# One-hot products for tiles 28 to 30 at the seam between attention and experts, and another order on VectorE

## The reference

```python
x = x + hilbert_attention(layernorm(x), Wqkv, bqkv, Wproj, bproj, mapping)       # part 1
x = x + cross_attention(layernorm(x), ctx, Wq, Wkv, null_kv, Wout, scale, bias)  # part 2: 16 heads, 154+1 keys
f = layernorm(x)                                                                 # part 3
probs = softmax(f @ Wr + br); gate = max(probs); idx = argmax(probs)             # 8 experts
pos = cumsum(one_hot(idx)) * one_hot(idx)        # place of a token in its expert's list
keep = pos < 512                                 # capacity 4096 / 8
expert_in[e, pos] = gate * f                     # "dispatch"
h = relu(expert_in @ W1 + b1); eo = h @ W2 + b2
x = x + gate * eo[idx, pos]                      # where kept, else x
```

## Time and profile before

| | us |
|---|---|
| median of 3 runs | 1298.02 (1295.5 to 1300.58) |
| the profiled execution, its own time | 1294.91 |
| its span | 1293.2 |
| PE busy | 1268.1 (98%) |
| DVE busy | 939.7 (73%) |
| ACT busy | 662.4 (51%) |
| POOL busy | 419.9 (32%) |

### The profile page before, as it was taken

One profiled execution on the slowest core, in us unless ns is written; L12 is line 12 of the kernel. 1 busy time (PEld: TensorE's weight loads), 2 busy tenths in 40 slices (PEclk: granted clock), 3 DMA queues, 4 the chain that ended last, 5 costly groups with the idle time before them and its releaser, 6 DMA issues.

```text
span 1293.2 us, 31661 instructions
## 1 busy us (share of the span) xinstructions
PE 1268.1 (98%) x12348; PEld 1032.6 (80%) x12348; DVE 939.7 (73%) x1903; ACT 662.4 (51%) x1868; POOL 419.9 (32%) x477
## 2 busy tenths in 40 slices
PE   9999999999999999999999999999999998999998
PEld 8988677777777788888888888888888876888886
DVE  6559787888886776777777777787767787665563
ACT  4456333433333755656556565565555752654552
POOL 3213454545432021213232132312212222555453
PEclk9999999999999999999999999999999999999999
DMA  8542244444323201103021020120202103664630
GB/s 268 169 132 66 68 157 158 148 151 165 109 83 109 82 10 42 50 18 107 18 75 50 18 105 20 48 77 18 74 18 98 58 26 133 231 208 153 189 99 22
DMA packets 70257, 123.75 MB, mean 96 GB/s; under 512 B 12313, under 2 KB 21553, under 8 KB 70114
## 3 DMA queue, kind: packets, MB, share of 16 engines
q1 hardware_dynamic: 61794, 98.17, 22.8%
q0 software_dynamic: 8320, 23.62, 5.2%
HBM read 83.19 MB, written 42.07 MB: 97 GB/s over the span
## 4 chain that ended last, share of the span: by engine, by line
PE 85%; DVE 9%; ACT 3%; issue 2%; DMA 1%; SPq 1%; POOL 0%; DVEq 0%; POOLq 0%
PE bank L71 20%; PE bank L73 18%; PE bank L72 18%; PE bank L2371 6%; PE bank L2355 6%; PE bank L2394 4%; PE bank L2386 2%; PE bank L1306 2%; PE bank L1276 1%; PE bank L1250 1%; PE bank L2927 1%; PE bank L2445 1%; PE bank L2434 1%; DVE turned_l L1054 1%; DVE a_recip L1060 1%
## 5 line engine op out<-in xcount | busy, mean ns | idle before, releaser
L1655 ACT ACTIVATE b_prob<-bank,b_neg_top 128x155 f32<-128x155 f32 x496 | 186.7, 408 | 115.0 <-DVE b_neg_top L1871 115.0
L1871 DVE TENSOR_REDUCE b_neg_top<-bank 128x6 f32<-128x930 f32 (+1 forms) x93 | 94.2, 1013 | 64.2 <-PE bank L2371 64.2
L71 PE MATMUL bank<-turned_h,big_h 128*128 128x512 f32 x320 | 131.3, 410 | 1.4 <-DVE turned_l L2131 1.2
L73 PE MATMUL bank<-turned_h,big_l 128*128 128x512 f32 x320 | 125.4, 392 | 0.0
L72 PE MATMUL bank<-turned_l,big_h 128*128 128x512 f32 x320 | 124.8, 390 | 0.0
L71 PE MATMUL bank<-b_wo_h,b_ot_h 128*128 128x512 f32 x256 | 111.5, 436 | 1.9 <-ACT b_ws L1688 1.7
L2355 PEld LDWEIGHTS bank<-ident,b_prob 128*128 128x128 f32 x640 | 92.8, 190 | 22.1 <-issue 5.0
L2355 PE MATMUL bank<-ident,b_prob 128*128 128x128 f32 x640 | 104.0, 285 | 3.3 <-DVE b_pt L1888 2.2
L1655 ACT ACTIVATION_READ_ACCUMULATOR b_prob<-bank,b_neg_top 128x1 f32 x496 | 103.9, 209 | 0.0
L73 PE MATMUL bank<-b_wo_h,b_ot_l 128*128 128x512 f32 x256 | 101.1, 395 | 0.0
L72 PE MATMUL bank<-b_wo_l,b_ot_h 128*128 128x512 f32 x256 | 99.9, 390 | 0.0
(11 more groups left out here) (361 smaller groups left out, 3353.7 us busy)
## 6 DMA issues: line engine op xcount, KB each, us to landing
wide<-in_L_ffn_W_dram SPq DMA_DIRECT2D x16, 1024.0 KB, 5.4
slot_rows<-empty_row SPq DMA_DIRECT2D x8, 1032.0 KB, 5.4
a_xr<-in_x_dram SPq DMA_DIRECT2D x32, 256.0 KB, 2.8
x_scratch<-a_xr SPq DMA_DIRECT2D x32, 256.0 KB, 2.4
tiles<-x_scratch SPq DMA_DIRECT2D x32, 256.0 KB, 3.7
rows<-x_scratch SPq DMA_DIRECT2D x32, 256.0 KB, 3.4
out_dram<-rows SPq DMA_DIRECT2D x32, 256.0 KB, 2.0
rows<-slot_rows SPq DMA_DIRECT2D x7, 1032.0 KB, 8.4
```

Of the source, the lines that this page charges most:

```text
L71: pe.matmul(out, lh, rh, start=first, stop=False)
L73: return pe.matmul(out, ll, rh, start=False, stop=last)
L1655: last = act.activation(prob[:, n % 2, j, h:h + 2 * L2 - 1:2], burst_banks(n, b)[:, h, o:o + L2], ACT.Exp, bias=neg_top[:, n % 2, h, j:j + 1],
L1871: dve.tensor_reduce(neg_top[:, n % 2, :, first:end], burst_banks(n, b)[:, :, 0:(end - first) * L2].rearrange("p h (j k) -> p h j k", k=L2) ...
```

## The change

It does the following:
- `queries(1, 3)` is cut in two in step 1: the first six matmuls stand ahead of `turn_p(1, 4)`, the other six at the end.
- y-statistics and logits of tile 28 and `w_stats(29)` on DVE move from the end of step 30 into step 31, behind the copy of the second turn, ahead of `route_slots`.
- SP fetches the rows of expert 0 once tile 27's scatter is done, in step 32. Tiles 28, 29, 30 come in by one-hot products, high part and remainder, as tile 31 does (`own_norm` on ACT, `place_own` for the matrices: 0 and 1 on DVE, 2 on GpSimd; `own_rest` for the remainders: 0 and 1 on GpSimd, 2 on DVE; `pick_own` on PE).
- The scatter of tiles 28 to 30 moves behind that fetch, to GpSimd's step 33.
- `warm` shrinks from seven, a narrow one and two to one; the pieces 4 to 7 of DVE's `expert_split` move behind `first_rest`.

```diff
@@ SP
             if tiled(n - 2):
                 need(sp, s["x2_made"], n - 1)
                 sp.dma_start(out_tiles[:, n - 2, :], row(n - 2)).then_inc(x2_stored[(n - 2) % (2 * G)], 16)
+            if n == NT:
+                sp.wait_ge(s["scattered"], SENT[LAST - 1])
+                for k in range(G):
+                    sp.wait_ge(x2_stored[k], 16 * NT // (2 * G))
+                    sp.dma_start(rows[:, 0, k, :], slot_tiles[:, k, :]).then_inc(first_rows[k], 16)
@@
-        sp.wait_ge(s["scattered"], SENT[LAST])
-        for k in range(G):
-            sp.wait_ge(x2_stored[k], 16 * NT // (2 * G))
-            sp.dma_start(rows[:, 0, k, :], slot_tiles[:, k, :]).then_inc(first_rows[k], 16)
@@ GpSimd
+        def own_rest(k):
+            hold(pool, s["own_high"], k + 1)
+            pool.tensor_tensor(own_l[k], own[k], own_h[k].bitcast(F32), ALU.subtract).then_inc(s["own_low"], 1)
+
+        def place_own(k):
+            m = NT - G + k
+            hold(pool, s["routed"], LAST)
+            hold(pool, s["own_placed"], k)
+            pool.tensor_scalar(own_picked[k], numbers[:, :], token_f[:, m:m + 1], c4["slot4"][:, k:k + 1], ALU.subtract,
+                               ALU.is_equal).then_inc(s["own_placed"], 1)
@@
             if n == NT:
                 power("y", n - 1)
-                scatter(LAST - 1)
+                own_rest(0)
                 power("w", n)
+                own_rest(1)
                 return
             if tiled(n - 2):
                 power("y", n - 1)
             if n == NT + 1:
+                place_own(2)
 
                 for k in range(G):
                     hold(pool, first_rows[k], 16)
+                scatter(LAST - 1)
                 scatter(LAST)
@@ ACT
+        def own_norm(k):
+            need(act, s["route_step"], BASE[LAST - 1] + 13)
+            here = rows[:, (NT - 1) // G % 2, k, :]
+            act.activation(own[k], here[:, 0:D], ACT.Identity, bias=here[:, D + 2:D + 3], scale=here[:, D + 3:D + 4])\
+                .then_inc(s["own_normed"], 1)
+            need(act, s["own_normed"], k + 1)
+            act.activation(own_h[k], own[k], ACT.Copy).then_inc(s["own_high"], 1)
@@
                 turned_y(n - 2)
                 route_exp(LAST - 1)
+                own_norm(0)
                 w_copy(n - 1)
+                own_norm(1)
+                first_norm(0)
+                own_norm(2)
                 turned_y(n - 1)
+                first_norm(1)
+                first_norm(2)
                 route_exp(LAST)
-                first_norm(0)
-                first_norm(1)
+                first_norm(3)
...
-                first_norm(2)
-                first_norm(3)
@@ DVE, closing
             if t == 2:
-                need(dve, s["x2_made"], n - 1)
-                norm_stats("y", n - 1, row(n - 2), EPS1)
                 read_counts(NG - 2)
-            logits(n - 2)
-            if t == 2:
-                w_stats(n - 1)
+            else:
+                logits(n - 2)
@@ DVE, step
                 route_apart(LAST - 1)
+                place_own(0)
                 w_stats(n - 1)
-                expert_split(4)
-                expert_split(5)
+                place_own(1)
                 add_residual(n - 1)
                 need(dve, s["x2_made"], n)
                 norm_stats("y", n, row(n - 1), EPS1)
                 add_counts(LAST - 1)
-                expert_split(6)
-                expert_split(7)
+                own_rest(2)
                 logits(n - 1)
                 route_last()
                 for k in range(KD):
                     first_rest(k)
+                for k in range(4, 8):
+                    expert_split(k)
@@
+            if n == NT - 1:
+                need(dve, s["x2_made"], n - 2)
+                norm_stats("y", n - 2, row(n - 3), EPS1)
+                logits(n - 3)
+                w_stats(n - 2)
             if t == 3 and there(i - 1):
                 route_slots(i - 1)
@@ PE
+        def pick_own(k, part, ready):
+            need(pe, s["own_placed"], k + 1)
+            need(pe, ready, k + 1)
+            for c in range(KD):
+                pe.matmul(first_banks[c], part[k][:, c * P:(c + 1) * P], own_picked[k],
+                          start=k == 0 and part is own_h, stop=False,
+                          skip_group_check=True)
@@
                 output(n - 1, 5, 8)
-                warm(7)
+                ...
+                pick_own(0, own_h, s["own_high"])
+                pick_own(0, own_l, s["own_low"])
+                pick_own(1, own_h, s["own_high"])
                 turn_y(n - 1)
-                warm(1, 256)
+                pick_own(1, own_l, s["own_low"])
                 logits(n - 1)
-                warm(2)
+                turn_first(0)
+                turn_first(1)
+                turn_first(2)
+                warm(1)
                 count_last()
-                first_turns()
+                pick_own(2, own_h, s["own_high"])
+                pick_own(2, own_l, s["own_low"])
+                turn_first(3)
+                pick(mine_h, s["mine_high"])
+                pick(mine_l, s["mine_low"], True)
@@
-            if asked and t == 1 and i:
-                queries(i + 1, 1)
+            if asked and t == 1:
+                queries(i + 1, *((1, 0, KD) if i else (3, 0, 2)))
@@
             if asked and 0 < t < 3:
-                queries(i + 1, 2 * t + 1)
+                queries(i + 1, 2 * t + 1, 2 if t == 1 and i == 0 else 0, KD)
```

More of the change, by code:

```diff
@@ L145, in decoder_kernel @@
         floor = nc.sbuf_base
+        place["floor"] = floor
         prob = nc.alloc_sbuf_tensor_at("b_prob", [P, 2, PS, PAIR], F32, offset=floor)
@@ L1480, in cross_attention @@
              "route_step route_exp counted counts_read routed scattered expert_high expert_low first_normed "
-             "first_turned first_high first_low numbered placed mine_normed mine_high mine_low").split()
+             "first_turned first_high first_low numbered placed mine_normed mine_high mine_low "
+             "own_placed own_normed own_high own_low").split()
     s = {n: sem("b_" + n) for n in names}
@@ L1513, in cross_attention @@
     picked = lay("b_picked", [P, CAP], F32R, "wide", half + 28 * D)
+    own_h, own_l, own_picked = ([lay(f"b_own_{a}{k}", [P, D], F32R, "floor", 4 * D * (3 * j + k))[:, :] for k in range(3)]
+                                for j, a in enumerate(("h", "l", "picked")))
+    own = [lay("b_own0", [P, D], F32, "floor", 4 * D * 9)[:, :], lay("b_own1", [P, D], F32, "wide", half + 4 * D)[:, :],
+           lay("b_own2", [P, D], F32, "wide", half + 12 * D)[:, :]]
     def run(step):
@@ L2127, in route_last, with place_own, own_rest @@
             dve.sem_inc(s["routed"], 1)
+        def place_own(k):
+            m = NT - G + k
+            need(dve, s["route_step"], BASE[LAST - 1] + 21)
+            need(dve, s["numbered"], 2)
+            dve.tensor_scalar(own_picked[k], numbers[:, :], token_f[:, m:m + 1], c4["slot4"][:, k:k + 1], ALU.subtract,
+                              ALU.is_equal).then_inc(s["own_placed"], 1)
+        def own_rest(k):
+            need(dve, s["own_high"], k + 1)
+            need(dve, s["own_low"], k)
+            dve.tensor_tensor(own_l[k], own[k], own_h[k].bitcast(F32), ALU.subtract).then_inc(s["own_low"], 1)
         def first_rest(k):
@@ L2476, in warm @@
                 pe.matmul(s_banks[:, 0, 0:cols], ident[:, :], lns_b[:, 0:cols], start=True, stop=True)
-        def first_turns():
-            need(pe, s["w_evac"], NT)
-            need(pe, s["q_evac"], KI * (NG - 1))
-            need(pe, s["ot_low"], 2 * NT)
-            turn_first(0)
-            turn_first(1)
-            pick(mine_h, s["mine_high"])
-            turn_first(2)
-            pick(mine_l, s["mine_low"])
-            turn_first(3)
         def turn_first(k):
@@ L2493, in turn_first, with pick @@
             for c in range(KD):
-                last = pe.matmul(first_banks[c][:, k * P:(k + 1) * P], xn[:, k, c * P:(c + 1) * P], ident[:, :],
-                                 start=k == 0, stop=k == G - 1, is_transpose=True, skip_group_check=True)
-                if k == G - 1:
-                    last.then_inc(s["first_turned"], 1)
-        def pick(part, ready):
+                pe.matmul(first_banks[c][:, k * P:(k + 1) * P], xn[:, k, c * P:(c + 1) * P], ident[:, :], start=False,
+                          stop=False, is_transpose=True, skip_group_check=True)
+        def pick_own(k, part, ready):
[5 more added lines that the diff above has]
+                          skip_group_check=True)
+        def pick(part, ready, final=False):
             need(pe, s["placed"], 1)
@@ L2502, in pick @@
             for c in range(KD):
-                pe.matmul(first_banks[c], part[:, c * P:(c + 1) * P], picked[:, :], start=False, stop=False,
-                          skip_group_check=True)
```

(4 more changed lines are left out.)

3 lines of the change are left out of this document (added).

## The result

| | before | after |
|---|---|---|
| median | 1295.66 us | 1298.86 us |
| lowest to highest (20 runs each) | 1293.73 to 1300.58 | 1295.62 to 1305.74 |
| profiled execution, its span | 1294.91, 1293.2 | 1300.3, 1298.6 |

By it the change made the kernel slower by 2.7 us (1.4 to 4.0). I had forecast no change, -0.26 us. The time lies inside my range and inside the 0.5%, but the measurement tells the difference from nothing, and it is on the other side of my sum.

What follows compares the result with a forecast made beforehand. It took TensorE, busy 98% of the span at full clock, as the bound. Terms -1.06 + 1.9 - 1.3 + 0.2 summed to -0.26 us: 1294.65 us by the profiled execution, 1297.8 against the median; range 1293.5 to 1302.

Steps and rivals of the forecast that it cites:

- Step 1: Third burst of scores: six query matmuls moved ahead cover PE's whole wait for ACT, -1.06 us.
- The last step: Attention's tile 31: the 2.23 us stall goes, but turn_y(29) waits 4 us and the output product starts late, +1.9 us.
- R3: Rival: TensorE's clock falls to 1.2 GHz at the 4 us gap before turn_y(29), up to +7.0 us, 1304.8; chance 0.06.
- The tail: From the end of output(31) to expert 0's first product: 15.9 us against 17.25, -1.3 us.
- R4: Rival: base rows land late, ACT and PE wait, the tail stays as long as before, +1.3 us, 1299.1; chance 0.07.
- R2: Rival: POOL's pieces cost twice, each own_rest 2.6 us instead of 1.3, tail +1.3, total 1300.4 us; chance 0.15.
- POOL's matrix: One-hot matrix on GpSimd in the tail: priced at 0.73 us, between rows of 0.73 and 1.29.
- The start of the experts: After expert 0's first product: expert_split(4..7), 2.8 us, is hidden by VectorE's idle time, +0.2 us.
- R1: Rival: all gains arrive, turn_y(29) isn't held, tail -2.7, step 1 -1.06, together -6.0 us, 1292; chance 0.18.

Runs made afterwards that it cites:

- e8_split_late: Kernel before with only VectorE's expert_split pieces 4 to 7 moved behind first_rest; 1295.95 us against 1296.07 for before, ratio 0.9994.
- e9_late_scatter: Kernel before with three unused iota operations on GpSimd ahead of tile 31's scatter; 1302.17 us against 1296.07 for before, ratio 1.0043.
- e5_place_dve: Changed kernel with the third one-hot matrix on VectorE, behind tile 31's residual, instead of GpSimd; 1299.17 us against 1296.07 for before, ratio 1.0018.
- e6: Changed kernel with the remainders own_rest(0) and own_rest(1) on VectorE instead of GpSimd; 1300.22 us against 1296.07 for before, ratio 1.0025.
- e1: Changed kernel with VectorE's order of the last step as it was before; 1301.36 us against 1301.14 for before, ratio 1.0006.
- e3: Changed kernel with four filler matmuls on PE ahead of turn_y(29); 1304.3 us against 1301.14 for before, ratio 1.0018.
- e2: Kernel before with only VectorE's new order in the last step; 1303.31 us against 1301.14 for before, ratio 1.0017.

## Why the prediction was wrong

**Step 1 was right** (-1.06 forecast, -1.08 in the profile, -1.0 as a change by itself).

**The last step failed in its clock.** The order did what I said, at the price I said: copy at 1057.43, a 4.05 us stall released by the residual, +1.9 us. My sum took the clock at nothing, and R3 had a chance of 0.06 with a price of up to 7.0. It happened, 1.8 us of it: half speed over 6.8 us, much of which passed under VectorE's own chain, which sets the start of output(31), and output(31) itself was not hit. I had argued from one execution in which a stall of 2.23 us left the clock at 1.00; six of the eight profiles with that stall show otherwise. In the Trainium skill (TensorE: Matmul & The Clock Gate, "Why this matters for your kernels") idle gaps between bursts are warned of, and that was nearer to the runs than my 0.06.

**The tail was nearly right.** -0.91 measured, -1.3 forecast. The base rows came in time (R4 is out), and POOL's remainders took 1.27 and 1.28 us, not twice that (R2 is out). What is missing lies at the residual, from which I had expected 0.45 us: it ended 6.42 us behind the start of the last matmul of output(31) before and after alike, and the logits 8.88 us behind it in both. What the tail gained, it gained behind the logits.

**POOL's matrix was outside my bounds.** I took 0.73 us and bounded it by 1.29, from the nearest rows by number of tensor inputs; it took 2.09. Two scalars from SBUF and the rounding output are in neither of those rows; the remainders on POOL round their output too and took 1.27 us, so the rounding alone is not the reason. The 2.09 us did not hold up the last scatter in GpSimd's queue, which waited for the routing; with the matrix on VectorE the routing of tile 31 ended 0.27 us sooner. The Trainium skill (GPSIMD Engine Reference, "Engine selection") calls GpSimd roughly at line rate with one input; this row does not agree: the same operation took 0.54 us on VectorE.

**The start of the experts failed as a step.** I gave +0.2 us and looked at the splits, which e8_split_late clears. I had followed PE's and VectorE's path to the first product and stopped there. Expert 1's rows hang on another path: routing of tile 31, last scatter, second fetch of expert 0's rows, fetch of expert 1's. That path did not get shorter with the tail, so the product's 0.91 us came off its lead, and 0.3 us more through the later routing. There were 0.8 us of slack: before, D was 9.22, and the one-for-one part of the curve meets C = 14.14 at D = 10.02. At 10.95 the changed profile was 0.9 us beyond it, and c_gate's collision put 1.1 us on top, 2.0 us in all. e9_late_scatter shows by itself that less lead costs time; that the median of the changed kernel loses 2 us there is not shown, since e5_place_dve, with 1.3 of them back in its profile, has a ratio of 1.0018.

**R1** (all gains) is out, since turn_y(29) was held. Together: -1.08 + 3.72 - 0.91 + 2.01 = +3.7 us in the profile. The ratio says 2.7. The runs' clocks fit: 0.9957 over 20 runs of the changed kernel, 0.9978 over 99 runs of the kernel before in the three other groups. Within the kernels' own runs (257 of them) a clock lower by 0.001 goes with 1.1 us more, so 0.0022 goes with 2.4 us; that is a correlation, and it holds the waits that lower the clock too. It is not a second account beside the stages. Among the kernels with the one-hot tail the mean is low with the new order (0.9948 to 0.9957 in after, e5, e6) and higher with the old one (e1, 0.9968) or the filler (e3, 0.9977); but the order alone has 0.998, and e9_late_scatter, without order or tail, 0.9955.

Still open: why the fetch of expert 1's rows lands so unevenly, why the order alone does not lower the mean clock, and what share of the 2.7 us the clock and the start of the experts each have in the median, since the stages are those of one execution each.

## What to carry to other kernels

Follow an edit beyond the point where the path you priced ends. When one path into a stage gets shorter, look for the others that it had been hiding: here the rows of the next expert had 0.8 us of slack, and the gain of 0.91 us alone used it up. Don't move idle time of the matmul engine into one longer gap: with the same order, four filler matmuls in the gap made the stage 1.8 us shorter (though not the kernel). And take the clock from many executions before arguing that a gap is harmless.

## What the runs showed of the hardware

- The granted clock fell to the 1.2 GHz level behind every unfilled stall of 4.02 to 4.05 us in the last step (for 6.8 us in after, e5 and e6, for 3.4 us in e2), and behind a stall of 2.23 to 2.24 us in six profiles of eight (for 3.4 us). The kernel before had mean clocks from 0.995 to 1.0 in its own runs, so the same code does not always pay.
- A 128x512 operation with one input, two scalars and a rounding output took 2.09 us on GpSimd and 0.54 on VectorE.
- VectorE operations that met a GpSimd addition took 1.17 (128x3), 1.26 (a copy of 128x4), 1.61 and 1.75 us, instead of 0.16, 0.17, 0.75 and 0.69. That copy has one input, so it is not two inputs alone that make an operation wait.
